# Two layers of graph convolution on one core: the opening in another order

## The reference

```python
h = relu(layernorm(x))
m = relu(relu(concat(h[src], edge_attr) @ W_msg.T + b_msg) @ W_msg2.T + b2)
h_neigh = segment_sum(m, dst) / max(segment_count(dst), 1)
x = x + concat(h, h_neigh) @ W_apply.T + b_apply            # layer 0
h = relu(layernorm(x))
alpha = softmax of edge_weight within each dst segment
agg = normalise(segment_sum(alpha * h[src], dst))
x = x + layernorm(normalise(0.5 * (h @ W_self + b_self + agg @ W_nb + b_nb))) * gamma + beta   # layer 1
```

## Time and profile before

| | |
|---|---|
| median of 3 runs | 11080.0 us |
| the profiled execution | 11096.56 us |
| its span | 11094.3 us |
| TensorE matmuls busy | 5466.0 us (49%) |
| VectorE busy | 3712.2 us (33%) |
| ScalarE busy | 1123.0 us (10%) |
| GpSimd busy | 6148.5 us (55%) |
| TensorE's granted clock, mean | 0.658 of full |

### The profile page before, as it was taken

How to read it: one execution, slowest core, us unless ns; L and a number is a source line. 1 busy time by engine, 2 the same in 40 slices (tenths; PEclk the granted TensorE clock), 3 DMA queues, 4 the chain that set the end, 5 groups by cost and what they waited for, 6 DMA issues and landing times. The chain is left out here.

```text
span 11094.3 us, 113937 instructions
## 1 busy us (share of the span) xinstructions
PE 5466.0 (49%) x26549; PEld 4240.2 (38%) x26549; DVE 3712.2 (33%) x14115; ACT 1123.0 (10%) x2074; POOL 6148.5 (55%) x6486
## 2 busy tenths in 40 slices
PE   4566666656656566565666533333333333333335
PEld 3444444444444444444444433222222222222224
DVE  5233223222222222222222433333333333333336
ACT  2111111111111111111111200000000000000002
POOL 2555545555544444545455466666666666666664
PEclk8777777777777777777777655655555555555556
DMA  4222222222222222222212222221111111111112
GB/s 142 53 52 53 54 52 53 55 52 53 61 61 61 59 62 62 59 52 54 52 52 53 66 56 55 53 54 50 46 45 45 46 45 45 45 45 46 46 45 73
DMA packets 402851, 613.77 MB, mean 55 GB/s; under 512 B 171715, under 2 KB 261679, under 8 KB 401871
## 3 DMA queue, kind: packets, MB, share of 16 engines
q0 software_dynamic: 206336, 422.99, 14.7%
q1 hardware_dynamic: 183232, 183.30, 6.1%
q10 hardware_dynamic: 13200, 6.56, 0.2%
HBM read 576.45 MB, written 35.92 MB: 55 GB/s over the span
## 5 line engine op out<-in xcount | busy, mean ns | idle before, releaser
L497 POOL DMA_INDIRECT rows_ring<-p_table,idx x3224 | 3073.5, 953 | 3125.9 <-DMA idx<-in_src_ring 1657.7
L845 DVE TENSOR_TENSOR acc<-acc,bank 128x128 f32 x6448 | 1823.5, 283 | 6553.0 <-remote 3238.4
L497 POOL DMA_INDIRECT rows_ring<-h_table,idx x3224 | 3058.9, 949 | 1698.5 <-issue 927.2
L848 DVE TENSOR_SCALAR onehot<-iota,dloc,coef 128x128 f32<-128x128 f32 x4840 | 1697.2, 353 | 432.7 <-issue 374.2
L1018 PE MATMUL bank<-onehot,work 128*128 128x128 f32 x6448 | 1106.7, 327 | 1089.9 <-ACT work L570 579.6
L1018 PE MATMUL bank<-onehot,rows_ring 128*128 128x128 f32 x3232 | 772.2, 414 | 1737.5 <-DVE onehot L848 914.9
L1018 PEld LDWEIGHTS bank<-onehot,work 128*128 128x128 f32 x6448 | 1011.2, 239 | 1132.3 <-issue 736.7
L1018 PE MATMUL bank<-work,rows_ring 128*128 128x128 f32 x3216 | 752.4, 408 | 1362.7 <-DVE work L848 694.9
L1018 PEld LDWEIGHTS bank<-onehot,rows_ring 128*128 128x128 f32 x3232 | 666.3, 305 | 1840.5 <-issue 1028.4
L1018 PEld LDWEIGHTS bank<-work,rows_ring 128*128 128x128 f32 x3216 | 650.7, 300 | 1463.8 <-issue 818.4
L1018 PEld LDWEIGHTS bank<-wmat,work 128*128 128x128 f32 x6848 | 1125.1, 233 | 63.4 <-issue 24.1
(11 more groups left out here) (129 smaller groups left out, 1062.7 us busy)
## 6 DMA issues: line engine op xcount, KB each, us to landing
work<-in_edge_t SPq DMA_DIRECT2D x403, 256.0 KB
rows_ring<-p_table,idx POOLq DMA_INDIRECT x3224
rows_ring<-h_table,idx POOLq DMA_INDIRECT x3224
idx<-in_src_ring SPq DMA_DIRECT2D x404, 8.0 KB
ht_rows<-rows_ring SPq DMA_DIRECT2D x25, 256.0 KB, 2.4
p_table<-rows_ring SPq DMA_DIRECT2D x25, 256.0 KB, 2.5
work<-ht_rows SPq DMA_DIRECT2D x25, 256.0 KB
h_table<-work ACTq DMA_DIRECT2D x25, 256.0 KB
```

The source lines that it names most:

```text
L497: pool.indirect_dma_start(out=rows_ring[:, 16 * h + G * k + j, :], out_offset=None, in_=table[:, :], in_offset=bass.IndirectOffsetOnAxis(a ...
L845: dve.tensor_tensor(win, win, ps_sum[layer][k % slots][:, j * P:(j + 1) * P], ALU.add).then_inc(added, 1)
L848: ins = dve.tensor_scalar(hot_slots[layer][k % slots][:, j * P:(j + 1) * P], iota[:, :], dloc[:, ds(t, 1)], coef[:, ds(t, 1)], ALU.is_equa ...
```

## The change

x is loaded in nine parts of three batches. The first part, the bias rows, the second part and the weights go first; the destinations and the tile arrays last. VectorE starts with the bias parts. Statistics, variance, root and scale are made per part, one part ahead of the normalisation; three of a batch's four tiles are normalised by VectorE (now one multiply and add, with the shift -mean x scale), the fourth by ScalarE. Only then come the scans for the counts; the two reductions over 3224 columns that found whether a partition is of one destination become comparisons of its first and last (one column). The counts are stored as they are; the reciprocals are taken in `coef`, in 17 parts: 128 columns ahead of body 0, then 194 ahead of each of bodies 1 to 16. TensorE's two carries come behind the table, ScalarE clears `acc` in four pieces instead of three.

```diff
@@ sync
-            sp.dma_start(cnt_arrays[0], dst_halo).then_inc(S["counts_in_loaded"], 16)
-            sp.dma_start(xq[:, 0:parts[1], :], tiled(x, 0, parts[1])).then_inc(s_x[0], 16)
-            sp.dma_start(brow..., rows.partition_broadcast(P)).then_inc(S["weights_loaded"], 16)
-            for n in range(1, 4): ...
+            load_x(0)
+            sp.dma_start(brow..., rows.partition_broadcast(P)).then_inc(S["rows_loaded"], 16)
+            load_x(1)
             sp.dma_start(wmat[:, :, :], mats.rearrange("k p f -> p k f")).then_inc(S["weights_loaded"], 16)
             sp.dma_start(we_sb[:, :], we).then_inc(S["weights_loaded"], 16)
+            for n in range(2, len(PARTS0)):
+                load_x(n)
...
+            sp.dma_start(cnt_arrays[0], dst_halo).then_inc(S["counts_in_loaded"], 16)
             sp.dma_start(dloc[:, :].bitcast(I32), dst_tiles).then_inc(S["tile_arrays_loaded"], 16)
...
-                sp.wait_ge(S["scalars_ready"], 1 + 2 * PARTS * n)
+                sp.wait_ge(S["scalars_ready"], 2 * PARTS) if n else sp.wait_ge(S["counts_made"], 1)
@@ scalar
+            def root0(n):
+                act.wait_ge(S["var0_ready"], n + 1)
+                act.activation(columns(sc_a, PARTS0[n]), columns(var, PARTS0[n]), ACT.Sqrt, bias=eps[:, :], scale=1.0 / P).then_inc(S["root0_ready"], 1)
+            def table_p(c):
+                h = c % 2
+                if c < NBATCH:
+                    at = c * G + G - 1
+                    act.wait_ge(S["scale0_ready"], c // 3 + 1)
+                    if c >= 2:
+                        act.wait_ge(S["normed0_turned"], c - 1)
+                    act.activation(normed0[h][:, G - 1, :], xq[:, at, :], ACT.Identity, bias=mean[:, at:at + 1], scale=sc_a[:, at:at + 1]).then_inc(S["fourth0_ready"], 1)
+                # then relu of batch c-1 into ht0, and the copy of batch c-2 into p_out
...
+            root0(0)
+            for n, part in enumerate(PARTS0):
+                if n + 1 < len(PARTS0):
+                    root0(n + 1)
+                for c in part:
+                    table_p(c)
...
+            act.wait_ge(S["limits0_made"], 1)
+            clear(0, LEN + 2)
             act.wait_ge(S["counts_made"], 1)
+            clear(LEN + 2, 2 * LEN + 2)
+            clear(3 * LEN + 2, NP)
             act.wait_ge(S["dloc_ready"], 1)
             act.wait_ge(S["scalars_stored"], 16)
+            clear(2 * LEN + 2, 3 * LEN + 2)
@@ vector
+            def stats0(n):
+                dve.wait_ge(s_x[n], 16 if n < len(PARTS0) - 1 else 32)
+                for c in PARTS0[n]:
+                    for at in range(c * G, c * G + G):
+                        ins = dve.bn_stats(stat6[:, at, :], xq[:, at, :])
+                link(ins)
+                mu, v, me, mo, so = raw_stats(n, PARTS0[n])
+                link(dve.tensor_tensor(mu, me, mo, ALU.add))
+                dve.tensor_tensor(v, v, so, ALU.add).then_inc(S["var0_ready"], 1)
+            def norm0(n):
+                dve.wait_ge(S["root0_ready"], n + 1)
+                link(shift_and_scale(PARTS0[n]))
+                dve.sem_inc(S["scale0_ready"], 1)
+                for c in PARTS0[n]:
+                    if c >= 2:
+                        dve.wait_ge(S["normed0_turned"], c - 1)
+                    for t in range(G - 1):
+                        at = c * G + t
+                        ins = dve.tensor_scalar(normed0[c % 2][:, t, :], xq[:, at, :], sc_a[:, at:at + 1], mean[:, at:at + 1], ALU.mult, ALU.add)
+                    ins.then_inc(S["normed0_ready"], 1)
+            stats0(0)
+            for n in range(len(PARTS0)):
+                if n + 1 < len(PARTS0):
+                    stats0(n + 1)
+                norm0(n)
...
-            dve.reciprocal(cnt_arrays[3], cnt_arrays[3]).then_inc(S["scalars_ready"], 1)
...
+            inverse_cuts = [0, *range(128, T, 194)]
+            inverse = Order(dve, S["inverse_order"])
+            def invert_counts(n):
+                a, z = inverse_cuts[n], (*inverse_cuts[1:], T)[n]
+                inverse.link(dve.reciprocal(coef[:, a:z], coef[:, a:z]))
+            between = {n: lambda n=n: invert_counts(n) for n in range(1, len(inverse_cuts))}
...
+            invert_counts(0)
+            bodies(dve, layer0, between, beside=layer0_and_pre)
@@ tensor
             pe.wait_ge(S["constants_made"], 7)
-            carry(1, 0)
-            carry(2, 1)
...
                     pe.wait_ge(S["normed0_ready"], c + 1)
+                    pe.wait_ge(S["fourth0_ready"], c + 1)
...
+            carry(1, 0)
+            carry(2, 1)
             fill(0)
```

More of the change, by code:

```diff
@@ L301, in gnn @@
         PRE = at_step[-1] + 6
-        parts = [0, 24, 48, 72, NTF]
+        PARTS0 = [range(c, min(c + 3, NBATCH)) for c in range(0, NBATCH, 3)]
         @block.sync
@@ L521, in _ @@
             act.wait_ge(S["constants_made"], 7)
[L522 to L536, removed]
-                    act.activation(p_out[h], ps_m1t[h][:, :], ACT.Copy).then_inc(S["p_ready"], 1)
@@ L736, in back_over, with raw_stats, shift_and_scale @@
                 carried_scan(tot, same_after, fwd, ALU.mult, ALU.add, 0.0, True, n)
[L738 to L742, removed]
[L743 to L760 removed]
+            def raw_stats(n, chunk):
+                me, se, mo, so = (stat6[:, chunk[0] * G:(chunk[-1] + 1) * G, j] for j in (1, 2, 4, 5))
+                mu, v = columns(mean, chunk), columns(var, chunk)
+                link(dve.tensor_tensor(mu, me, mo, ALU.subtract))
+                link(dve.scalar_tensor_tensor(v, mu, P / 4.0, mu, ALU.mult, ALU.mult))
+                link(dve.tensor_tensor(v, v, se, ALU.add))
+                return mu, v, me, mo, so
+            def shift_and_scale(chunk):
+                r, mu = columns(sc_a, chunk), columns(mean, chunk)
+                link(dve.reciprocal(r, r))
+                return dve.scalar_tensor_tensor(mu, mu, -0.5, r, ALU.mult, ALU.mult)
+            dve.wait_ge(S["rows_loaded"], 16)
             link(dve.tensor_tensor(b["b_self"], b["b_self"], b["b_nb"], ALU.add))
@@ L784, in _ @@
+            dve.sem_inc(S["limits0_made"], 1)
+            forward(cnt_arrays, cnt_eq[:, 0:LEN], onec[:, :].to_broadcast([P, LEN]), ALU.mult, ALU.add, 0.0, 1)
+            back_over(cnt_arrays, 1)
+            dve.sem_inc(S["counts_made"], 1)
             dve.wait_ge(S["tile_arrays_loaded"], 48)
@@ L867, in x1_scale @@
             def x1_scale(n, chunk):
-                r, mu = columns(sc_a, chunk), columns(mean, chunk)
                 dve.wait_ge(S["root1_ready"], n + 1)
-                link(dve.reciprocal(r, r))
-                dve.scalar_tensor_tensor(mu, mu, -0.5, r, ALU.mult, ALU.mult).then_inc(S["scale1_ready"], 1)
+                shift_and_scale(chunk).then_inc(S["scale1_ready"], 1)
             def x1_step(s):
@@ L905, in _ @@
             dve.wait_ge(S["coef_filled"], FILLS)
-            dve.wait_ge(S["sums_zeroed0"], 3)
-            bodies(dve, layer0, [*zip(at_step, steps), (at_step[-1] + 3, clear_last_tiles)], beside=layer0_and_pre)
+            dve.wait_ge(S["sums_zeroed0"], 4)
+            inverse_cuts = [0, *range(128, T, 194)]
[4 more added lines that the diff above has]
+            between = {n: lambda n=n: invert_counts(n) for n in range(1, len(inverse_cuts))}
+            for at, step in [*zip(at_step, steps), (at_step[-1] + 3, clear_last_tiles)]:
+                between[at] = (lambda step=step, n=at: (invert_counts(n), step())) if at in between else step
+            invert_counts(0)
+            bodies(dve, layer0, between, beside=layer0_and_pre)
             def four_of(arr, c):
```

72 lines of the change are left out of this document (31 added, 41 removed).

## The result

In 20 runs each, taken in turn on one chip, the changed kernel took a median of 11069.48 us (11023.98 to 11094.19) and the kernel before 11089.58 us (11070.59 to 11114.97): a ratio of 0.9977 [0.9966, 0.9988], 25 us less (13 to 38); the two medians alone lie 20 us apart. The forecast was 32 us less. The result lies inside the forecast's range and inside its "no change" of 0.5%. The profiled execution took 11069.99 us with a span of 11067.7, so the span is 26.6 us shorter than the 11094.3 of before.

The account below looks back on a forecast made before the run. Two gather loops are the kernel, no engine full in layer 0's; the edited opening is 179 us. Gains of 29 (TensorE's start) and 4 (body 0) less 1 (parts) make 32: 11080 to 11048 us, range 10990 to 11095.

Parts of the forecast that it names:

- Rows at 8, bias 5.1, statistics: Opening: bias rows land at 8 us, bias work takes 5.1, statistics of part 0 end at 17, part 1 at 21.
- Cycle per part 7.0 us: Table making: VectorE takes 7.0 us per part of three batches, with ScalarE's fourth at 6.1 us fitting barely.
- rival C: ScalarE's added fourth and deeper order hold the table at 3.3 us a batch; gain 8 to 12, 11070 us; chance 0.10.
- VectorE held from 35 to 42: Table making: VectorE waits from 35 us because the first stores queue behind the loads; the backlog runs on after 42.
- Done at 84: VectorE finishes the table at 84 us (79 to 94), 51 earlier; 81 summed plus 3 for late turns.
- Scans and gathers: Beside the counts: each 6.9 us scan lets about one gather through; some 11 issued by 131, the other 21 by 157.
- Cover 18 us; cost nothing: Body 0: TensorE needs the last group at 175, the gathers end at 157, so held gathers cost nothing.
- Body 0 in 20 us: TensorE's start to the next gather, 23.9 us before, gets 4 us shorter (0 to 10), with most rows landed.
- The parts, cost 1 of 22: Reciprocals in 17 parts ahead of VectorE's first 17 bodies: 22 us of VectorE work, 1 us cost (0 to 22).
- Rival B: Split boundaries in VectorE's first bodies hold up TensorE; at 4 us each 64 us cost, 11111 us; chance 0.07.
- Layer 0's pace: Layer 0's loop, first matmul to first gather of h_table, stays at 6081 us within 40.
- rival A: Faster by over 0.5%: early bodies or a loop's pace give 23 us beyond the sum; about 11000 us; chance 0.25.

Follow-up runs that it names:

- the late loads: Changed kernel with destinations loaded behind batch 10's stores, tile arrays and table base behind the whole table; ratio to the kernel before 0.996 [0.9947, 0.9973].
- 16 empty boundaries: Changed kernel with one reciprocal ahead of the store and empty splits of VectorE's loop ahead of bodies 1 to 16; ratio to the kernel before 0.9974.
- seventeen times the work: Changed kernel with each of the 17 part reciprocals done 17 times in a row; ratio to the kernel before 1.0119 [1.0098, 1.0139].
- Cut into single bodies: Changed kernel with VectorE's layer 0 loop split ahead of each of bodies 1 to 50, nothing at the new splits; ratio to the kernel before 0.9951.
- the kernel on the fifth chip: Changed kernel with later loads and VectorE's loop split ahead of each of bodies 1 to 50; 8326.39 us against 8365.05 for the kernel before, 0.9954.
- five times: Changed kernel with each of the 17 part reciprocals done five times in a row; ratio to the kernel before 0.9985 [0.997, 1.0].

## Why the prediction was right, step by step

- *Rows at 8, bias 5.1, statistics.* The rows came at 7.45, the bias parts end at 12.5, part 0's statistics at 16.2 (forecast 17), part 1's at 19.6 (21). Right.
- *Cycle per part 7.0 us.* It is 6.35 (62.54 to 68.89). Twelve bn_stats take 2.41, a pitch of 0.20, where the 16 of the earlier trace rows had 0.254; that row was the wrong one to carry over, and why it is longer wasn't looked into. ScalarE kept up, so rival C is out.
- *VectorE held from 35 to 42.* It was held from 33.2 to 44.6. The place and the cause were right, as the late loads show; the wait was 4 us longer.
- *Done at 84.* It was 81.7. The four cycles began at 49.8, not 47, and took 25.5, not 28, so that they ended at 75.3 as summed (75). The rest took 6.4 (6.1); the 3 us added for late turns were the error. That this "can't be much better" than the 82 of DMA alone was wrong: DMA is at 249 GB/s from 40 to 82, not at the 310 of the sum, stores run on behind VectorE's end, and with the late loads VectorE is done at 72.5. "DMA busy without a hole" was wrong too (a share of 0.78).
- *First gather 93* was 91.6. *Scans 42.3:* 81.74 to 124.06 is 42.3. *Counts to first matmul 23.5:* 124.14 to 147.82 is 23.7. *TensorE's start 149.8* was 147.8, so 31.2 us were gained where 29 were forecast.
- *Scans and gathers.* 11 gathers were through by 128.5 and the last was issued at 153.8; the forecast was 11 by 131 and the last at 157. Six of them took 3.3 to 7.3 us. By the Trainium skill (SBUF — State Buffer, "SBUF: two separate sides"), of a VectorE instruction with two SBUF inputs and a GpSimd one that reads SBUF, whichever starts first holds the shared ports and the other is blocked. The trace agrees with the first half of this: GpSimd was held for the whole VectorE instruction. The other half is not seen: the half scan at 120.48 starts with a gather in flight (116.97 to 121.19) and takes 3.58 us, as that of the earlier trace rows with none about; the mask at 103.00 starts with one in flight to 103.72 and takes 3.52, as the comparison at 81.74. The 14 us of delay that it would have brought didn't come.
- *"Cover 18 us; cost nothing".* This is the step that the runs don't bear out. The held gathers cost TensorE's start nothing, but they moved the last gather from some 131.6 (91.6 and 32 of 1.25 us) to 154.8, 7 us behind TensorE's start, and on these chips body 0 stalls until they are out. With all of them out, body 0 takes 14.3 us, so that body 1 would start at 147.8 + 14.3 = 162.1 instead of 168.7: an estimate of 6.6 us, from the table above.
- *Body 0 in 20 us.* It took 20.9, 3 us gained where 4 were forecast. The reason given, gathers still being issued, is borne out on the slower chips by the table, and not on the fifth, where they don't hurt. That "TensorE's start sets the loop's start" is half of it: body 1 follows the later of TensorE's start and the last gather. The last gather came 33.7 us earlier (188.43 to 154.75), TensorE's start 31.2, and both were forecast at about these sizes; so the 34.2 us at body 1 don't tell the two paths apart, and that the sum left one of them out and still fits is luck.
- *The parts, cost 1 of 22.* It fits where it can be read: 40.1 against 40.0 us a body where nothing else disturbs, some 2 us for 17. On the slower chips it lies under the scatter. Rival B is out: 16 empty boundaries cost nothing that shows, and seventeen times the work costs half of itself. (Its price of 11111 us is 0.28% above before, so it would have been inside "no change"; the 0.07 for "slower by more than 0.5%" was too much.) Cut into single bodies, the loop took 1884 us for bodies 17 to 50 against 1907 and more. The Trainium skill (Runtime: NRT & Kernel Launch, "Instruction fetch mechanics") prices a taken branch and not straight code. The difference has the sign that this would give, in one execution each, and no run shows the cause.
- *Layer 0's pace.* The loop took 6087 us instead of 6081. From body 1 on 9 us were lost again. On the other chips the changed kernel took 12 us less there than the kernel before (5919 against 5931, one execution each, on two chips), and its variants from 29 less to 39 more. Bodies of the same code scatter between executions on the three chips by 18 us (17 to 50) and 49 us (50 to 100), more than these 9. That may be why a gain of 34 us at body 1 reads as 25 in one comparison and as 40 in another. The 23 us beyond the sum of rival A didn't come.

What stays open: what the "remote" and "issue" stalls are, and why gathers being issued bring them on four chips and not on the fifth. In front of VectorE's sums they come to 4981 to 5463 us in all thirteen profiles on the slower chips and to 9 us in the one on the fifth, and no edit here moved them. Loading of code is a rival that the trace speaks against. The DMA view of the changed kernel has these two queues for instructions (packets, MB, share):

```profile
q8 instruction: 31, 0.51, 0.0%
q14 instruction: 63, 0.52, 0.0%
```

94 packets in all face 1751 waits of the two kinds in front of VectorE's sums alone; the kernel on the fifth chip moved 114 and has 27. That these queues show every load of code is not known.

## What to carry over

Take an opening apart by when each engine can start, not by what each is busy with: here loads in need order let the table be made 53 us earlier, and work with no reader waiting (scans, reciprocals) was put where another engine was the slower. What it does to its neighbours still counts: here the scans held the gathers. A chain shortened in front of a loop is worth its microseconds only up to the next thing that is late, here the last gather; check body 1, not the first matmul. And where an execution scatters by more than the edit is worth, show the edit by its stage in the profile, and multiply it until it shows, as the parts at seventeen times did; at five times they were still lost in it.

## What the runs showed of the hardware

- One kernel, unchanged, took 11090 us on one chip, 10922 to 10939 on three and 8365 on a fifth, with no chip's runs spread over more than 0.7%. The opening was the same within 2.5 us on the two chips where it was profiled. What differs in the rows is the idle time called "remote" and "issue" in the loops. TensorE's granted clock, a mean over its two levels, was 0.93 of full on the last chip between 2000 and 3000 us, with 835 us busy, and 0.72 on the first, with 616. In layer 1 it was lower on the last chip (0.52 against 0.56), and the stage was 728 us shorter all the same, so the clock doesn't make the difference there.
- A gather that starts during a VectorE scan, subtraction or mask on two inputs ends 0.7 to 0.9 us behind it (scan of 6.93 us: 7.34 us for the gather); beside a reciprocal of 20.3 us gathers keep their 0.94 us. VectorE's own instruction isn't longer for it (3.58 and 3.52 us).
- On the four slower chips body 0 took 14.1 to 14.3 us where GpSimd had issued all its gathers before TensorE began, and 18.9 to 34.2 where it hadn't; on the fifth 14.2 although it hadn't.
